# A spare buffer moved in front of the FFN's activations: the matmul's two operands change places modulo 512 bytes

## The reference

```python
x = x + 0.5 * ffn(layernorm(x))
x = x + attn(layernorm(x))
x = x + 0.5 * ffn(layernorm(x))

# ffn: a shared expert over all tokens, and 8 routed experts, top 2 of each token
shared = silu(x @ sg) * (x @ su) @ sd            # inner width 2048
...                                              # rmsnorm, router, softmax, top 2, weights w
xg = xf[dispatch]                                # 8 experts, up to 640 tokens each
gate = silu(einsum('ech,ehi->eci', xg, rg)); up = einsum('ech,ehi->eci', xg, ru)
eout = einsum('eci,eih->ech', gate * up, rd)     # inner width 1024
...                                              # weighted, added to the tokens
# attn: qkv, rmsnorm of q and k, 16 heads of 16, causal in groups of 64 tokens, projection
```

## The kernel before, in words

| buffer | start | modulo 512 |
|---|---|---|
| x | 0 | 0 |
| w1 (2 x 8 x 768 x 4 bytes) | 32768 | 0 |
| stage, constants, small statistics | 81920 to 95792 | various |
| zh, zl (8192 bytes each) | 95808, 104000 | 64 |
| sg_s, h_s, hh, hl (4096 each) | 112192, 116288, 120384, 124480 | 64 |
| zn (8480) | 128576 | 64 |
| pad_w0 (160) | 137056 | |
| w0 (49152), or attention's aw over it | 137216 | 0 |
| azh, azl (attention) | 192512, 193536 | 0 |
| yh, yl (attention) | 210112, 211136 | 192 |

## Time and profile before

### The profile page before, as it was taken

How to read it: one execution, slowest core, us unless ns; L and a number is a source line. 1 busy time by engine, 2 the same in 40 slices (tenths; PEclk the granted TensorE clock), 3 DMA queues, 4 the chain that set the end, 5 groups by cost and what they waited for, 6 DMA issues and landing times.

```text
span 2165.6 us, 38424 instructions
## 1 busy us (share of the span) xinstructions
PE 2130.2 (98%) x14228; PEld 1950.4 (90%) x14228; DVE 1427.1 (66%) x3137; ACT 1029.7 (48%) x2006; POOL 465.9 (22%) x443
## 2 busy tenths in 40 slices
PE   8999999999999999999999999999999999999999
PEld 7888899999998788888888888888999999988888
DVE  7666556666664788888898986665466666633333
ACT  3233335555553666666666663333355555533222
POOL 4323211122112222222224322332112121200000
PEclk9999999999999999999999999999999999999999
DMA  9231225464445000000101101322244444441010
GB/s 276 81 124 57 74 62 137 128 153 100 100 112 157 20 1 20 21 20 1 35 1 57 38 11 68 110 65 74 66 100 106 113 103 100 112 136 57 32 59 20
DMA packets 194602, 168.41 MB, mean 78 GB/s; under 512 B 17017, under 2 KB 175149, under 8 KB 194416
## 3 DMA queue, kind: packets, MB, share of 16 engines
q1 hardware_dynamic: 176752, 144.57, 22.0%
q0 software_dynamic: 17664, 21.38, 5.6%
HBM read 104.32 MB, written 68.07 MB: 80 GB/s over the span
## 4 chain that ended last, share of the span: by engine, by line
PE 86%; DVE 9%; issue 3%; ACT 1%; SPq 1%; POOL 0%; DMA 0%; another core or an unknown queue 0%; DVEq 0%; ACTq 0%; POOLq 0%
PE gate_up_p L339 28%; PE quad L339 24%; PE out_p L377 21%; PE misc L377 4%; PE misc L512 2%; PE quad L529 1%; DVE p_s L1176 1%; PE quad L543 1%; PE misc L403 1%; DVE smax L1172 1%; PE misc L395 1%; DVE y_s L1185 1%; DVE h_s L1042 1%; DVE vv L1152 1%; PE misc L414 1%
## 5 line engine op out<-in xcount | busy, mean ns | idle before, releaser
L339 PE MATMUL gate_up_p<-zh,w 128*128 128x512 f32 (+2 forms) x2368 | 706.3, 361 | 2.9 <-DVE h_s L1042 2.3
L713 ACT CAST hh<-h_s 128x512 fp32r<-128x512 f32 (+2 forms) x511 | 276.1, 540 | 714.8 <-DVE h_s L1042 658.1
L377 PE MATMUL out_p<-w,hh 128*128 128x256 f32 x2808 | 557.5, 281 | 4.9 <-DVE hl L1058 4.3
L339 PE MATMUL quad<-zh,w 128*128 128x512 f32 (+2 forms) x1728 | 483.2, 347 | 0.0
L339 PEld LDWEIGHTS gate_up_p<-zh,w 128*128 128x128 f32 x2368 | 429.0, 188 | 53.8 <-DVE h_s L1042 3.8
L377 PEld LDWEIGHTS out_p<-w,hh 128*128 128x128 f32 x2808 | 457.2, 189 | 17.6 <-DVE hl L1058 7.6
L339 PE MATMUL gate_up_p<-zl,w 128*128 128x512 f32 (+2 forms) x1184 | 421.1, 356 | 0.0
L377 PE MATMUL out_p<-w,hl 128*128 128x256 f32 x1404 | 392.5, 280 | 0.0
L1058 DVE TENSOR_TENSOR hl<-h_s,hh 128x512 fp32r<-128x512 f32 (+2 forms) x431 | 247.9, 575 | 135.5 <-ACT hh L713 119.5
L339 PEld LDWEIGHTS quad<-zh,w 128*128 128x128 f32 x1728 | 309.2, 188 | 25.1
L1042 DVE TENSOR_TENSOR h_s<-gate_up_p,sg_s 128x512 f32<-128x512 f32 (+2 forms) x296 | 178.4, 603 | 231.2 <-PE gate_up_p L339 213.2
(11 more groups left out here) (201 smaller groups left out, 2802.5 us busy)
## 6 DMA issues: line engine op xcount, KB each, us to landing
stage<-in_L_ffn_rg SPq DMA_DIRECT2D x128, 128.0 KB
stage<-in_L_ffn_ru SPq DMA_DIRECT2D x128, 128.0 KB
stage<-in_L_ffn_rd SPq DMA_DIRECT2D x128, 128.0 KB
slots_d<-empty SPq DMA_DIRECT2D x16, 662.5 KB, 6.9
zh_d<-zh SPq DMA_DIRECT2D x16, 512.0 KB
zl_d<-zl SPq DMA_DIRECT2D x16, 512.0 KB
y_d<-x SPq DMA_DIRECT2D x16, 512.0 KB
zh<-zh_d SPq DMA_DIRECT2D x16, 512.0 KB, 4.1
```

The lines of the kernel that those rows point to most:

```text
L339: last = pe.matmul(dst, a, b, start=(k == 0), stop=(k == 3 * n - 1))
L377: last = pe.matmul(out[:, j // 2, o:o + C], a[:, par, cols], w[:, hi, :], start=(c == 0 and i == 0 and j % 2 == 0), stop=(c == NCH - 1 and ...
L713: nc.scalar.copy(hh[:, n % 2, 0:ncol], h_s[:, n % 2, 0:ncol]).then_inc(sm["hh_done"], 1)
```

## The change

The buffer `zn` is declared ahead of `zh` and not behind `hl`, followed by a new pad of 96 bytes, and the pad in front of `w0` shrinks from 160 bytes to 64. All else is as before.

```diff
         tmeta = sb("tmeta", [P, 4, MAXT], I32)
 
+        zn = sb("zn", [P, 2, BT, ROW], F32)
+        sb("pad_z", [P, 24], F32)
         zh = sb("zh", [P, 2, KC, SB], F32R)
         zl = sb("zl", [P, 2, KC, SB], F32R)
         sg_s = sb("sg_s", [P, 2, SB], F32)
         h_s = sb("h_s", [P, 2, SB], F32)
         hh = sb("hh", [P, 2, SB], F32R)
         hl = sb("hl", [P, 2, SB], F32R)
-        zn = sb("zn", [P, 2, BT, ROW], F32)
-
-        sb("pad_w0", [P, 40], F32)
+
+        sb("pad_w0", [P, 16], F32)
         ffn_mem = ExitStack()
         w0 = sb("w0", [P, 2, NCH, PIECE], F32R, ffn_mem)
```

## The result

The changed kernel took 2174.03 us (median of 4 runs, 2171.36 to 2176.98), the one before 2160.91 (4 runs, 2157.47 to 2163.46): a ratio of 1.0068 (95% interval 1.0055 to 1.0082), 0.7% slower. The forecast was 2166 with a range of 2142 to 2186. The time lies inside it, on the side that had 0.31. Against the likeliest case it is off: +13.1 us came where +3.1 was forecast and that case allowed +11 at most.

A forecast was written before the change was run, and what follows sets the result against it. TensorE's matmul pace was taken as the bound; -6.7 and -3.7 us for down, +5.4 and +8.1 for gate and up gave +3.1 on 2162.6, rounded to 2166 us, range 2142 to 2186.

The forecast's parts named there:

- the likeliest case: Gate, up and down matmuls exchange the costs of their address relations: +3.1 us, between -5.0 and +11.1; chance 0.35.
- the side that had 0.31: Whole kernel: the chance given to a time slower by more than about 0.3%, 6.5 us.
- The bound and the quantity: Whole kernel: TensorE busy for 98% of the span, so only the pace of back-to-back matmuls is left to change.
- The addresses: Six buffers, zh to hl, move up by 8576 bytes, from 64 to 448 modulo 512; w0, w1 and attention stay.
- The layout that does nothing: Rival, all matmuls: differences in pace have nothing to do with addresses; time 2163, chance 0.08.
- Modulus 512: Start addresses of moving and loaded operands were compared modulo 512 bytes: z and h at 64 before, 448 after.
- Each relation takes its cost with it: Gate and up take down's relation and its cost, down takes theirs: -6.7, -3.7, +5.4 and +8.1 us.
- the exchange: Expert stage, 256 columns: down goes to 277 to 278 ns, gate and up to 281; whole case has chance 0.35.
- The 512-column matmuls: Gate and up, 3072 matmuls: +3.5 ns each or nothing, half taken; expected at 392 to 396 ns.
- 384 columns: Gate and up, 1536 matmuls: +3.5 ns each or nothing, half taken; expected at 336 to 340 ns.
- A nanosecond of duration is a nanosecond of pace: Wherever TensorE is full, 1 ns in a group's mean duration was taken as 1 ns in pace.
- The rival on the slow side: Gate and up, starting 64 bytes behind the load, stall at 398 ns for 512 columns: +19.6 us, 2182; chance 0.24.

The follow-up runs named there:

- e1: Against the kernel before: zn in front of z, with a longer pad that keeps z and h 64 bytes past the weights; ratio 0.9997.
- e4: Against the kernel before: only the last pad grew from 160 to 288 bytes, moving w0 and not z, h or w1; ratio 1.0042.
- e12: Against the kernel before: same order, 256 bytes of pad in front of z, z and h 320 bytes past both weights; ratio 0.9995.
- e3: Against the kernel before: only h moved to 64 bytes below the weights, z stayed 64 past; ratio 1.0039.
- e10: Against the kernel before: z at none and h 64 below against w1, z 64 past and h at none against w0; ratio 1.0069.

## Why the prediction was right and wrong

- **The bound and the quantity** were right. TensorE's pace was what made the time longer, with the other engines' busy time within 1%. The waits were not still: they shrank and took up part of the +20 us.
- **The number** lay in the range because the range was wide enough for all rivals (2142 to 2186), not because the sum was right. The slower matmuls came to +20 us where +3.1 was forecast, and only 9 (between the two traces, the clock allowed for) to 13 (between the medians) of them reached the time.
- **The addresses** were right as worked out, and that it is the distance modulo something that acts is shown by e1, e4 and e12. The layout that does nothing (0.08) is out, and with it what was drawn from the rule that was set beside it, of the Trainium skill, "TensorE: Matmul & The Clock Gate", section "Part 2: What happens when you issue a matmul", that the weight load takes no bandwidth from the running matmul. The traces disagree with that: 1395 matmuls against 1370 in the same 240 us, with one pad longer and z and h in their place. They don't show what is taken from which.
- **Modulus 512** was taken over from the change's own words and never tested against a row. The period is 256. For this change it makes no difference: 64 past and 64 below are different distances either way.
- **"Each relation takes its cost with it"** is the step that failed. It seemed to hold in the expert stage at 256 columns: 281 to 279 for down, 277 to 281 for gate_up_p. But there the quad group, which has the same distances, went the other way, and the exchange was nearly nil in the pace: down -0.3 ns (-0.6 us in place of -6.7), gate and up +0.4 (+0.7 us in place of +5.4). It failed in the shared blocks, where down was to gain 1.2 ns and lost 2.0 (+6.3 us in place of -3.7). e3 and e10 show why: gates with an unchanged distance went from 229 to 233 ns when only h moved. The price belongs to the pair, z's distance with h's, and two rows of one family under one distance don't give the price of the other family under it. Attention's `aw,yl`, 278 to 281 ns with both operands in place, is the same effect as far as can be told; the prediction would have taken it as a sign of wrong addresses.
- **The 512-column matmuls** were mis-sized: +1.75 ns allowed, half of a bound of 3.5; measured +3.5 ns, +10.9 us in place of +5.4. The prediction named this as the place where it would break. The bound came from 256-column rows; this shape is longer, and its price lay at the bound.
- **384 columns** came out as said (+2.7 us, forecast +2.7).
- **A nanosecond of duration is a nanosecond of pace** was not exact. With the change durations of 512 columns rose from 391 or 392 to 394, 2 or 3 ns, and the pace by 4.3 (229.0 to 233.3 in the last stage). The prediction's 392 to 396 for the profile looked fulfilled, while the loss per matmul was half as large again.
- **The rival on the slow side** came nearest in direction: gate and up slower, with down slower too. But by its own mark it doesn't decide: over all 6144 gate and up matmuls the loss is 14.3 us, 2.3 ns on average, below its 2.8 (3.5 at 512 columns alone), and the gates stood at 394 ns, not at 398. Its reason is not borne out: a moving stream that starts just below the load is no special case. With 64 below w0 the last stage took 307.0 us, with 128 below 307.5 and with 32 past 307.3.

What stays open is the mechanism under the pattern. The runs show what it depends on (distance modulo 256, for both families together, and what ran ahead) and not what collides, nor why the steps at the lower clock are even in all kernels. Relations among attention's own operands were not moved against each other.

## What to carry to other kernels

Where TensorE is full and each matmul has a weight load beside it, the distance of the moving operand from the loaded one, modulo 256 bytes, was worth up to 1% of the time here, and any edit that adds or moves a small buffer can change it by accident: pin it with pads, and hold it fixed when something else is measured. Test the distances of all families that follow one another together, as whole kernels; prices measured for one family don't add up. Read pace from starts, or from the number of matmuls in a window at full busy time, not from busy time or duration.

## What the runs showed of the hardware

- At the full clock the pace of back-to-back matmuls with weight loads follows a pattern that repeats within 1 ns from chunk to chunk and from kernel to kernel. It depends on the operands' distances; one layout can have two patterns (233 233 234 and 236 231 236 231 in the changed kernel's first stage). Lowest seen in long runs: 227 ns for 512 columns, 113 for 256; usual in slow patterns 233 and 118 to 120.
- No distance was the fastest for settled gates (227 ns) and among the slowest for down (120 ns), so it is not simply the worst relation.
- At the lower clock the steps took 426 to 427 ns for 512 columns (14 traces) and 213 to 214 for 256 (6 traces), at every distance seen there. A stretch there costs less than its share: a step of 512 columns takes 427 ns against 227 to 233, 1.8 to 1.9 times.
- Distances of -192 and 64, 192 and -64, -128 and 128, 256 and 0 have the same patterns. A kernel at 320 took the time of one at 64 (0.9995, 0.9986 to 1.0004).
- An operand that didn't move can run 4 ns slower per matmul (229 to 233) because a neighbouring product's operand did.
- Behind attention's stage, in which TensorE waits now and then, the granted clock fell to the lower level (1.2 GHz) for a part of 20 us in some executions (0.74 over 1310 to 1330 us in that of before, 1.00 in that of after), worth 4.6 us between two profiles of a change worth 13.
